# Identity matmuls without a use, issued by TensorE where three later stages of a four-stage model begin

## The reference, cut to what matters

```
x = x + tanh(g_xattn[0]) * gated_attention(norm(x), ctx)       # 16 heads of 128, fp8 weights, two attentions
x = x + tanh(g_ffn[0])   * mixture_of_experts(norm(x))         # 32 experts, 8 chosen per row, SiLU
x = x + tanh(g_xattn[1]) * channel_attention(norm(x), ctx)     # 16 batches, 8 heads of 8 channels
x = x + tanh(g_ffn[1])   * nvfp4_mlp(norm(x))                  # 2048 wide, 4-bit weights, GELU

# mixture of experts
probs = softmax(h @ router_w.T);  rw, sel = top_k(probs, 8);  rw = rw / sum(rw)
out   = sum over experts e of  (silu(h @ w_gate[e]) * (h @ w_up[e])) @ w_down[e] * weight_of(e)

# channel attention, for one batch and head (q from norm(x), k and v from ctx, 8 channels by 256)
out = softmax(q.T @ k / sqrt(8)) @ v.T
```

## Time and profile before

| | |
|---|---|
| median of 3 runs | 1088.36 us (1087.72 to 1088.56) |
| profiled execution, its time | 1089.46 us |
| its span, first to last instruction | 1087.7 us |
| mean granted TensorE clock | 0.947 |
| busy: PE, DVE, ACT, POOL | 981.8, 749.8, 539.2, 268.0 us |

### The profile page before, as it was taken

How to read it: one execution, slowest core, us unless ns; L and a number is a source line. 1 busy time by engine, 2 the same in 40 slices (tenths; PEclk the granted TensorE clock), 3 DMA queues, 4 the chain that set the end, 5 groups by cost and what they waited for, 6 DMA issues and landing times. The chain is left out here.

```text
span 1087.7 us, 19039 instructions
## 1 busy us (share of the span) xinstructions
PE 981.8 (90%) x6752; PEld 822.5 (76%) x6752; DVE 749.8 (69%) x1301; ACT 539.2 (50%) x1655; POOL 268.0 (25%) x416
## 2 busy tenths in 40 slices
PE   3689999999999999956899999995999999699998
PEld 3579999999999998855677777773666665577776
DVE  8858878777878787776544454445688888666653
ACT  5566666666666665622433333323455554233332
POOL 2133333333333333302422222202010111323130
PEclk8799999999999999976799999997899998799999
DMA  5001020101010100004111111001000000110001
GB/s 180 1 2 59 2 59 2 59 2 59 2 60 1 60 4 18 2 1 176 44 47 47 47 46 46 3 0 59 1 1 0 0 0 2 58 59 30 29 0 39
DMA packets 22823, 35.40 MB, mean 33 GB/s; under 512 B 2016, under 2 KB 19552, under 8 KB 21600
## 3 DMA queue, kind: packets, MB, share of 16 engines
q1 hardware_dynamic: 22464, 34.38, 9.6%
q10 hardware_dynamic: 288, 0.10, 0.0%
HBM read 33.42 MB, written 1.05 MB: 32 GB/s over the span
## 5 line engine op out<-in xcount | busy, mean ns | idle before, releaser
L251 PE MATMUL ps<-wt_hi,xq 128*128 128x256 f32 (+1 forms) x512 | 124.7, 278 | 13.0 <-issue 10.3
L251 PE MATMUL ps<-wt_lo,xq 128*128 128x256 f32 (+1 forms) x512 | 122.2, 281 | 0.0
L458 ACT ACTIVATE square<-ps 128x128 bf16<-128x128 f32 x384 | 100.6, 293 | 39.7 <-PE ps L251 39.6
L251 PEld LDWEIGHTS ps<-wt_hi,xq 128*128 128x128 f32 x512 | 98.4, 192 | 17.2 <-issue 15.3
L1624 ACT ACTIVATE ca_probs<-ps 128x512 f32<-128x512 f32 x128 | 69.5, 595 | 82.8 <-PE ps L1544 82.8
L251 PEld LDWEIGHTS ps<-wt_lo,xq 128*128 128x128 f32 x512 | 98.9, 193 | 0.0
L1684 DVE TENSOR_REDUCE context_mx<-ps 128x4 f32<-128x1024 f32 x64 | 76.9, 1201 | 26.4 <-PE ps L1516 26.4
L596 POOL TENSOR_TENSOR rstd<-rstd,half_neg 128x6 f32<-128x6 f32 x64 | 87.2, 1362 | 5.0
L1210 POOL TENSOR_TENSOR moe_w_lo<-moe_w_all,moe_w_hi 128x384 fp32r<-128x384 f32 x48 | 54.8, 1176 | 135.4 <-ACT moe_w_hi L1311 135.4
L458 ACT ACTIVATION_READ_ACCUMULATOR square<-ps 128x1 f32 x384 | 86.0, 225 | 0.0
L1375 DVE TENSOR_TENSOR moe_act_g<-moe_act_g,ps 128x512 f32<-128x512 f32 x48 | 33.0, 687 | 70.5 <-PE ps L1246 70.5
(11 more groups left out here) (225 smaller groups left out, 2685.8 us busy)
## 6 DMA issues: line engine op xcount, KB each, us to landing
moe_w_all<-in_experts SPq DMA_DIRECT2D x8, 1152.0 KB, 5.4
wp_rows<-in_wproj SPq DMA_DIRECT2D x16, 256.0 KB, 2.9
ffn_codes<-in_codes SPq DMA_DIRECT2D x8, 384.0 KB, 3.2
ffn_w_scales<-in_code_scales SPq DMA_DIRECT2D x8, 384.0 KB, 3.9
w_rows<-in_wq SPq DMA_DIRECT2D x8, 256.0 KB, 3.7
w_rows<-in_wqx SPq DMA_DIRECT2D x8, 256.0 KB, 3.9
w_rows<-in_w_kv_x SPq DMA_DIRECT2D x16, 128.0 KB, 3.6
x_rows<-in_x SPq DMA_DIRECT2D x2, 512.0 KB, 5.1
```

Of the source, the lines that this page charges most:

```text
L251: last = mm(ps[:, first + bank, col:col + n], left[:, c, tokens], w[:, c, wcol:wcol + n], start=(j == 0), stop=(j == len(steps) - 1))
L458: last = nc.scalar.activation(square[:, j, :], ps[:, bank, (j % 4) * P:(j % 4) * P + P], ACT.Square, scale=float(HD) ** -0.5, accum_out=su ...
```

## The change: what it does

A helper `keep_busy(nc, k, bank, count)` issues `count` matmuls on TensorE: stationary operand `ident`, moving operand `ident` repeated four times (512 columns of plain float32), result in one PSUM bank in which nothing is kept at that place. They wait for nothing and release nothing, and what follows them on TensorE stands in the queue behind them. There are 24: three at the end of `gated_attention`; five at the start of `mixture_of_experts` and three ahead of the transposes of the router's weights; five ahead of the first `replicate` of `channel_attention` and one after each `row_scores` of the first batch; two at the start of `nvfp4_mlp` and two between the two halves of its transposes.

```
+def keep_busy(nc, k, bank, count):
+
+    for _ in range(count):
+        nc.tensor.matmul(k.ps[:, bank, :].rearrange("p (r n) -> p r n", r=4), k.ident[:],
+                         k.ident[:].unsqueeze(1).broadcast_to([P, 4, P]), start=True, stop=True)
@@ gated_attention, tensor, end
             outputs(u, GROUPS - 1)
+            keep_busy(nc, k, 2, 3)
@@ TurnedNorm.tensor
         for j in range(2 * CH):
             half, c = divmod(j, CH)
+            if self.interleaved and j == CH:
+                keep_busy(nc, k, 7, 2)
@@ gated_mlp, tensor
             mm = nc.tensor.matmul
+            keep_busy(nc, k, G_BANK, 5 if moe else 2)
             turn.tensor(pe)
...
                     if first:
+                        keep_busy(nc, k, R_BANK, 3)
                         router.tensor_turn(pe)
@@ channel_attention, tensor
+            keep_busy(nc, k, 7, 5)
             pe.wait_ge(s["h_low"], 1)
             replicate(0, 0, 0, first=True)
...
                 row_scores(0, 0, pair, first=(pair == 0))
+                keep_busy(nc, k, 7, 1)
                 if pair == 0:
                     replicate(0, 1, 0)
```

## The result

| | before | after |
|---|---|---|
| median | 1088.46 us | 1081.97 us (1080.94 to 1082.94, 4 runs) |
| ratio | | 0.9941, 95% interval 0.9924 to 0.9959 |
| profiled execution | 1089.46 us, span 1087.7 | 1081.08 us, span 1079.3 |
| mean granted clock | 0.947 | 0.971 |

The change makes the kernel 6.5 us faster; 9.3 was forecast. The times of after form two groups, near 1081.0 (clock 0.971) and near 1082.9 (clock 0.968). The profile is of the first group; why there are two is not known.

A forecast was written before the change was run, and what follows sets the result against it. TensorE was taken as the bound inside the loops, with waits and half clock at stage beginnings. The terms, 3.5 + 6.8 - 1.0 = 9.3 us less than the median 1088.36, gave 1079.1 us, range 1074.5 to 1084.5.

The forecast's parts named there:

- Price of a filler: One added matmul of 512 plain float32 columns on TensorE: 0.85 us at 2.4 GHz, 1.71 us at 1.2 GHz.
- Attention's end and experts' beginning: Start of the mixture of experts: fillers hidden in waits, faster transposes and logits, loop entered at full clock; 3.5 us less.
- One sign: Ahead of the router's transposes: three fillers end at 526.0, 0.7 us after the router is ready, and end last.
- Channel attention: Start of channel attention: head and first batch at full clock, 6.8 us less.
- the partial rival: Clock held only in part: channel attention gives about 3, total 1083, or experts 0 to 1.8, 1081 to 1083; chance 0.20.
- the head's term: Channel attention ahead of its first batch: replicates, four pairs and two transposes cheaper at full clock; 2.5 us less.
- The first batch: Channel attention's first batch: 14.32 us against 9.79 for a later one, 4.5 less, 0.2 left for VectorE's large low part.
- Last stage: Start of the last stage: two fillers ahead of ready transposes at half clock, two between the halves; 1.0 us more.
- The sum: Whole kernel: 3.5 + 6.8 - 1.0 = 9.3 us less, 1079.1 us against the median.
- Slower: Mainly the five fillers at the experts' start: they run at half clock and are the wait; 10.5 more, 1098.9; chance 0.08.
- all: Whole kernel: all half-clock work comes back, 31 us halved to 15.5, less 1.0 in the last stage; 1073.9; chance 0.06.
- nothing: Whole kernel: fillers fit the waits but do not hold the clock; 1088; chance 0.06.

The follow-up runs named there:

- The part alone: Kernel before plus only the experts' fillers (three at attention's end, five at the block's start, three ahead of the router's transposes): 1084.24 us, ratio 0.9954.
- 4.9 alone: Kernel before plus only channel attention's fillers (five ahead of the first replicate, one behind each row scores of the first batch): 1084.87 us, ratio 0.9955.
- the singles: The four fillers, one behind each row scores of the first batch; changed kernel without them, the five ahead of the first replicate kept: 1086.81 us, ratio 0.9986.
- 1.7 alone: Kernel before plus only the two and two fillers at the start of the last stage: 1090.78 us, ratio 1.0016.
- Without the bridge: Changed kernel without the three fillers at attention's end, the five at the experts' start kept: 1081.59 us, ratio 0.9954.

## Why the prediction was right, and where it was not

- **Price of a filler.** 0.85 us at full clock, two records: as forecast. Three more ahead of the router's transposes cost 2.7 us.
- **Attention's end and experts' beginning.** 3.5 us forecast, 3.6 in the landmarks. The steps came nearly as told: the transposes released by VectorE, the clock kept (1.00 until 510.5), a fall while the logits run, the loop entered at full clock. One sign did not: the fillers ahead of the router's transposes were to end 0.7 us after the router and end together with it. The logits ended 1.6 us earlier and not 1.9 (six more at full spacing, not nine), and the router 1.5, counted from attention's end. The part alone measured 5.0 us (interval 3.5 to 6.5).
- **Channel attention.** This is the term that was mis-sized: 6.8 forecast, 4.4 in the landmarks and 4.9 alone. The head gave 0.9 instead of 2.5, since the clock fell in the pairs, as the partial rival had it at 0.20, though for some 3 us only. At full clock the head's term was right: in the run with one filler more between the replicates, paid with 0.2, the head took 2.3 us less than before. The first batch gave 3.4 instead of 4.3: its wait for the large low part on VectorE is 0.74 us where I had left 0.2. That the clock's hold needs the singles is shown by taking them out.
- **Last stage.** 1.0 more forecast; 1.9 in the landmarks, 1.7 alone (0.8 to 2.7). The clock was thought to be back for the second pair of fillers; they took 1.96 us, most of it still at half. The mechanism and sign were right, and the size was half of what came.
- **The sum.** By landmarks 6.0 us (3.6, 4.4 and -1.9, before rounding) stand against 9.3; the medians say 6.5. The forecast was 3 us too high: 2.4 in channel attention, 0.9 in the last stage.
- **Slower, all, nothing.** The five fillers began at full clock, so the slower rival's condition didn't come in the profiled execution. Without the bridge two runs of seven were at the time of before; whether its condition came in them is not known, since they have no trace.
- **What I did not price.** The clock's fall comes at different moments of the same code from execution to execution. It moved attention by 1.7 us between two traces, the first batch between 10.9 and 15.4, and the last stage's loop by 1.5.

## What to carry to other kernels

Work without use pays where TensorE waits ahead of its own work on the path, and only if it ends before the releaser: count the wait in the trace, divide by the price of one filler, and leave the rest open; ahead of work that is ready at once it is a plain cost (the last stage here). Several short waits in a row may need a filler in each: without the four singles the clock fell in the pairs and stayed down for nearly all of the batch behind them. Where a stage ends, look at what else must end before the next block: TensorE's tail was 2.5 us shorter and the block began 0.4 earlier, since GpSimd was then last. Compare such a change over several runs and by landmarks of a stage, since the clock falls at different places of the same code.

## What the runs showed of the hardware

- The same instructions in the same order, with 0.7 us waits between them, kept 2.4 GHz in one execution and fell to 1.2 in another (first batch of channel attention: 10.88 us in the changed kernel, 15.4 in the one without the last stage's fillers).
- After an idle stretch of 3.61 us the fillers still ran at 2.4 GHz, in the profiled execution without the bridge (4.53 us for five).
- Identity times identity, mostly zeros, left the clock at 1.00 while they ran (498.8 to 503.7 and 521.6 to 524.2 in the changed kernel).
- The clock fell while TensorE was busy without a gap, on 48 matmuls of 32 columns, in every trace, with fillers ahead of them or not, and also with fillers among them. In the changed kernel it fell 2.7 us into the run of them (507.86 to 510.6), which a wait of 0.70 us precedes.
